# Decoder layer on one core: expert rows gathered five tiles ahead, and the long convolution's products formed from cyclic copies

## What is computed

```python
x = x + attn(layernorm(x))
# convolution: 32 heads of 8 channels, 256 taps, k = v = ctx, q = layernorm(x)
kv  = einsum('bhil,bhjl->bijhl', k_, v_)           # 8 x 8 products a head, symmetric in i, j
y   = causal_conv(kv, ssm_kernel) + kv * D         # each product along the sequence
out = einsum('bijhl,bhil->bjhl', y, q_)            # sum over i against q
x = x + out
# experts: top 2 of 8 by a softmax router
for e in range(8): inter += where(sorted_ids == e, rows, 0) @ expert_gate_up[e]
h = up * silu(gate);  out_rows = h @ expert_down[e];  out.at[token].add(out_rows * score)
x = x + out
```

## Time and profile before

| | us |
|---|---|
| median of 3 runs | 1803.71 (1803.37 to 1810.03) |
| the profiled execution, its own time | 1810.99 |
| its span, first to last instruction | 1809.1 |
| convolution: first matmul of the heads to the last, both groups | 743.1 to about 1134.9 |
| experts: first row transposes to the last down product | 1304.3 to 1797.6 |
| busy: PE, DVE, POOL, ACT | 1513.5, 1141.0, 712.3, 678.5 |

### The profile page before, as it was taken

The page is one execution under the profiler, slowest core; times in us unless marked ns, Lnnn a source line. Parts: engine busy times, 40 slices in busy tenths (PEclk is TensorE's granted clock), DMA queues, the critical chain, the costliest instruction groups (busy, mean ns, idle before and its releaser), DMA issues. The chain is left out here.

```text
span 1809.1 us, 34128 instructions
## 1 busy us (share of the span) xinstructions
PE 1513.5 (84%) x8665; PEld 1192.7 (66%) x8666; DVE 1141.0 (63%) x3591; ACT 678.5 (38%) x1818; POOL 712.3 (39%) x1160
## 2 busy tenths in 40 slices
PE   4999999999999997799968888667187888878886
PEld 4888888888888885666656666567155555555554
DVE  5788777777777776699989999866422222222221
ACT  3777677767676776100001000023122222222222
POOL 2111111111111101688846888266633343344343
PEclk9999999999999999999989999655599999899999
DMA  5543333433343445411131111369534444344441
GB/s 168 122 106 95 94 93 93 110 94 93 95 109 92 109 97 216 151 46 47 46 116 36 47 45 34 128 162 259 128 66 74 76 72 73 66 78 79 72 79 35
DMA packets 89767, 172.13 MB, mean 95 GB/s; under 512 B 26384, under 2 KB 26384, under 8 KB 88656
## 3 DMA queue, kind: packets, MB, share of 16 engines
q1 hardware_dynamic: 63584, 122.46, 25.3%
q0 software_dynamic: 18176, 35.80, 11.0%
q10 hardware_dynamic: 7920, 12.93, 2.8%
HBM read 78.10 MB, written 44.79 MB: 68 GB/s over the span
## 5 line engine op out<-in xcount | busy, mean ns | idle before, releaser
L1097 PE MATMUL ps_y<-pairs,taps 128*128 128x288 f32 x1280 | 324.5, 410 | 35.4 <-DVE prods L1170 32.1
L1097 PEld LDWEIGHTS ps_y<-pairs,taps 128*128 128x128 f32 x1280 | 238.3, 190 | 121.1 <-POOL pairs L1041 41.6
L853 ACT ACTIVATE probs<-neg_scores,neg_max 128x256 f32<-128x256 f32 x512 | 255.2, 505 | 26.1 <-DVE neg_max L654 25.9
L1170 DVE TENSOR_TENSOR prods<-ps_y,q_g 128x224 f32<-128x224 f32 (+7 forms) x960 | 251.3, 402 | 17.7 <-issue 8.0
L654 DVE CUSTOM_DVE_ANT_0 neg_scores<-ps_scores,alibi 128x256 f32<-128x256 f32 x512 | 194.8, 418 | 91.0 <-PE ps_scores L519 60.4
L1041 POOL TENSOR_TENSOR pairs<-ctx_g 128x32 f32 (+11 forms) x512 | 215.5, 460 | 43.0 <-PE ps_y L1097 31.8
L1513 POOL DMA_INDIRECT out<-y_row,back x72 | 113.2, 1573 | 293.1 <-ACT y_row L1705 158.3
L1894 DVE TENSOR_TENSOR st_lo<-ps_x,st_hi 128x512 fp32r<-128x512 f32 x72 | 49.8, 691 | 249.2 <-ACT st_hi L1690 249.2
L863 ACT ACTIVATE probs_t<-ps_probs_t 128x512 f32<-128x512 f32 x208 | 124.0, 596 | 130.5 <-PE ps_probs_t L530 130.4
L530 PE MATMUL ps_probs_t<-ident,probs 128*128 128x128 f32 x1024 | 159.2, 279 | 8.9 <-ACT probs L853 8.9
L1588 PE MATMUL ps_x<-ident,srow 128*128 128x128 f32 x288 | 49.1, 296 | 121.0 <-DMA srow<-xn_rows,take 120.8
(11 more groups left out here) (185 smaller groups left out, 3287.2 us busy)
## 6 DMA issues: line engine op xcount, KB each, us to landing
q_stack<-q_hi SPq DMA_DIRECT2D x128, 128.0 KB, 2.3
k_stack<-k_hi SPq DMA_DIRECT2D x128, 128.0 KB, 2.3
taps<-kernel_pad SPq DMA_DIRECT2D x64, 256.0 KB, 3.1
x_in<-in_x SPq DMA_DIRECT2D x16, 512.0 KB, 3.5
q_stack<-q_lo SPq DMA_DIRECT2D x64, 128.0 KB, 2.3
k_stack<-k_lo SPq DMA_DIRECT2D x64, 128.0 KB, 2.3
x_rows<-x_mid SPq DMA_DIRECT2D x16, 512.0 KB, 3.0
ctx_g<-in_ctx_t SPq DMA_DIRECT2D x2, 4096.0 KB, 12.4
```

Source lines behind the costliest of these rows:

```text
L853: last = act.activation(probs[h % 2][:, tt, :], neg_scores[h % 2][:, tt, :], ACT.Exp, bias=neg_max[par][:, h, tt:tt + 1], scale=-1.0, accu ...
L1097: last = pe.matmul(ps_y[par][:, lc, 0:GB * PAIRS], taps[r][:, block_cols:block_cols + P], pairs[par][:, mc, :, :], start=(mc == 0), stop=( ...
L1170: last = dve.tensor_tensor(prods[par][:, :, :, to:to + n, term], y[:, :, :, col:col + n], head_of(q_g, own, q_from, n), ALU.mult)
```

## The change

**Experts.** RING goes from 8 to 12, the rows have six buffers (`ROW_BUFS`) instead of four, and the gather runs five tiles ahead (AHEAD = 5) instead of three. The scatter of tile n now always waits for the landing of tile n-2, and for that of tile n-1 only where the two tiles have different experts: a table `tile_wait_i`, made by three more DVE instructions at the end of routing (and a constant made by POOL and DVE at its start), gives the value to wait for, which POOL loads into a register for each tile.

**Convolution.** The ring of eight is laid out twice in a row, so that a ring row that wraps is contiguous. Three tiles are new, each with two buffers: `ctx_ring` and `q_ring` (the head's eight values twice) and `y_rows` (each ring row of y continued by the values that a later row needs). ACT fills them: `turn_ctx` one copy, `keep_y` one copy for `q_ring` and three from `ps_y` for `y_rows`. POOL's `form_pairs` is two multiplications, of 1024 and 128 elements. DVE's `multiply` is four, of 1280 and three times 256 elements, from `y_rows` and `q_ring`; the result is term by term. DVE's `halve` adds terms 4 to 7 onto 0 to 3 (1024 elements), POOL's `fold` adds 2 onto 2 (512) and then 1 onto 1 (256), and signals `z_ready`. PE waits for ACT's copy (`y_kept`) where it waited for DVE.

```diff
                 def form_pairs(g, k, par):
                     pool.wait_ge(y_ready, k * 2 + (g * SH + par + 1 - 2 + Y_START))
-                    for col, i, j, n in pair_segments():
-                        last = pool.tensor_tensor(pairs[par][:, :, :, col:col + n],
-                                                  head_of(ctx_g, k * 2 + par, i, n),
-                                                  head_of(ctx_g, k * 2 + par, j, n), ALU.mult)
-                    last.then_inc(pairs_ready, 1)
+                    wait_apart(pool, ctx_ring_ready, k * 2 + (g * SH + par + 1), passed)
+                    own = by_lane(ctx_g, k * 2 + par)
+                    to = pairs[par][:, :, :, :].rearrange("p m b q -> p (m b) q")
+                    pool.tensor_tensor(to[:, :, 0:HALF * SD].rearrange("p n (d i) -> p n d i", i=SD),
+                                       own.unsqueeze(2).to_broadcast([P, EC * GB, HALF, SD]),
+                                       turned(ctx_ring[par], HALF), ALU.mult)
+                    pool.tensor_tensor(to[:, :, HALF * SD:PAIRS], own[:, :, 0:HALF], own[:, :, HALF:SD], ALU.mult)\
+                        .then_inc(pairs_ready, 1)
...
-                    wait_apart(pool, prods_ready, k * 2 + (g * SH + par + 1 + PRODS_START), passed)
-                    first = prods[par][:, :, :, :, 0:FOLD]
-                    pool.tensor_tensor(first, first, prods[par][:, :, :, :, SD - FOLD:SD], ALU.add).then_inc(folded, 1)
+                    h = k * 2 + (g * SH + par)
+                    wait_apart(pool, halved, h + 1, passed)
+                    pool.tensor_tensor(prods[par][:, :, 0:2, :], prods[par][:, :, 0:2, :], prods[par][:, :, 2:4, :], ALU.add)\
+                        .then_inc(folded, 1)
+                    wait_apart(pool, folded, h + 1, passed)
+                    pool.tensor_tensor(by_lane(q_g, k * 2 + par), prods[par][:, :, 0, :], prods[par][:, :, 1, :], ALU.add)\
+                        .then_inc(z_ready, 1)
...
-                    pe.wait_ge(prods_ready, h + (1 - 2 + PRODS_START))
+                    pe.wait_ge(y_kept, h + (1 - 2 + KEPT_START))
...
+                def keep_y(g, k, par):
+                    h = k * 2 + (par + g * SH)
+                    act.wait_ge(prods_ready, h + (1 - 2 + PRODS_START))
+                    ring_of(q_ring[par], q_g, k * 2 + par)
+                    act.wait_ge(y_ready, h + (1 + Y_START))
+                    y = ps_y[par][:].rearrange("p c (b q) -> p (c b) q", b=GB)
+                    near = y[:, :, 0:HALF * SD].rearrange("p n (d i) -> p n d i", i=SD)
+                    rows = y_rows[par]
+                    whole_rows = rows[:, :, 0:HALF * ROW].rearrange("p n (d r) -> p n d r", r=ROW)
+                    act.activation(whole_rows[:, :, :, 0:SD], near, ACT.Copy)
+                    act.activation(whole_rows[:, :, 0:HALF - 1, SD:ROW], near[:, :, 1:HALF, SD - HALF + 1:SD], ACT.Copy)
+                    act.activation(rows[:, :, HALF * ROW:ROWS].rearrange("p n (u i) -> p n u i", u=2),
+                                   y[:, :, HALF * SD:PAIRS].unsqueeze(2).to_broadcast([P, EC * GB, 2, HALF]),
+                                   ACT.Copy).then_inc(y_kept, 1)
...
+                    with act.Fori(0, SH // 2 - 1) as k:
+                        for par in range(2):
+                            keep_y(g, k, par)
+                            turn_ctx(g, k + 1, par)
...
                 def multiply(g, k, par):
-                    dve.wait_ge(y_ready, h + (1 + Y_START))
+                    dve.wait_ge(y_kept, h + (1 + KEPT_START))
                     dve.wait_ge(z_ready, h + (1 - 2 + Z_START))
...
+                    dve.tensor_tensor(prods[par][:, :, 0:HALF + 1, :], main_rows(y_rows[par], HALF + 1),
+                                      turned(q_ring[par], HALF + 1), ALU.mult)
+                    for e in range(HALF + 1, SD):
+                        d = SD - e
+                        last = dve.tensor_tensor(prods[par][:, :, e, :], y_rows[par][:, :, d * ROW - d:d * ROW - d + SD],
+                                                 q_ring[par][:, :, e:e + SD], ALU.mult)
                     last.then_inc(prods_ready, 1)
 
-                def add_up(g, k, par):
-                    wait_apart(dve, folded, k * 2 + (par + g * SH + 1), passed)
-                    dve.tensor_reduce(head_of(q_g, k * 2 + par, 0, SD), prods[par][:, :, :, :, 0:SD - FOLD], AX_X,
-                                      ALU.add).then_inc(z_ready, 1)
+                def halve(g, k, par):
+
+                    h = k * 2 + (par + g * SH)
+                    wait_apart(dve, prods_ready, h + (1 + PRODS_START), passed)
+                    dve.tensor_tensor(prods[par][:, :, 0:HALF, :], prods[par][:, :, 0:HALF, :], prods[par][:, :, HALF:SD, :],
+                                      ALU.add).then_inc(halved, 1)
...
-        RING = 8
+        RING = 12
         BUFS = 4
-        AHEAD = 3
+        ROW_BUFS = 6
+        AHEAD = 5
...
-                    if not (first_round(kk) and r == 0):
-
-                        wait_apart(pool, y_scattered[(r - 1) % BUFS], turn(kk, r - 1) * 16 + 16, passed)
+                    if not (first_round(kk) and r < 2):
+
+                        wait_apart(pool, y_scattered[(r - 2) % BUFS], turn(kk, r - 2) * 16 + 16, passed)
+                    if one_back:
+
+                        wait_apart(pool, y_scattered[(r - 1) % BUFS], landed, passed)
```

More of the change, by code:

```diff
@@ L1284, in build_decoder @@
                 back = [sb_in(tiling, f"back{i}", [P, 1], U32) for i in range(RING)]
[L1285 removed]
+                srow = [sb_in(tiling, f"srow{i}", [P, E]) for i in range(ROW_BUFS)]
                 st = [[sb_in(tiling, f"st_{part}{i}", [P, EC, P], F32R) for part in ("hi", "lo")] for i in range(2)]
@@ L1330, in build_decoder @@
             take_ready = sem("take_ready")
-            row_load = [sem(f"row_load{i}") for i in range(BUFS)]
+            row_load = [sem(f"row_load{i}") for i in range(ROW_BUFS)]
             st_done = sem("st_done")
```

116 lines of the change are left out of this document (75 added, 41 removed).

## The result

The kernel after takes 1946.22 us (median of 4 runs, 1944.21 to 1951.73), the kernel before on the same chip 1805.16 (1803.37 to 1810.03): a ratio of 1.078, interval 1.075 to 1.081. The prediction was 1932. The profiled execution of the kernel after took 1945.0, its span is 1943.3.

What follows compares the result with a forecast made beforehand. DVE was taken to bound the convolution at 5.65 us a head, and PE with late gathers the experts. Convolution +225 and experts -97 give +128, 1939 on the profiled basis, 1932 us as a median; range 1850 to 1990.

Steps and rivals of the forecast that it cites:

- Part 1: Experts: gathers five tiles ahead are hidden, PE sets 5.4 us a tile instead of 6.75, 97 us less.
- Part 2, engine costs: Convolution, work a head: DVE 3.8 us, POOL 4.7, ACT 1.8, PE 5.1.
- The chain of two heads: Convolution: loop through fold, pairs, PE, ACT, multiply, halve and fold takes 16.3 us over two heads, 8.1 a head.
- The exclusion: Convolution: DVE and POOL instructions on SBUF tiles run in turns, 8.8 us a head with two handoffs.
- PE's clock: Convolution: PE's clock falls in idle time, so slower bursts add 0.4 us a head, bounds 0 to 1.4.
- The sum of a head: Convolution: 9.2 us a head against 5.65, 220 us more over 62 steps.
- (a): Convolution: no exclusion and the clock stays up, 8.0 us a head, 1857 us; chance 0.10.
- (b): Convolution: every PE burst starts at lower clock, or POOL's strided operands cost more; 9.9 a head, 1975 us; chance 0.22.
- (c): Experts: transfers in flight slow each other, step 6.4 us, gain only 25, 2004 us in all; chance 0.07.
- (d): Convolution: no exclusion, POOL folds while DVE halves, PE sets 5.2 us a head, 1684 us; chance 0.04.
- (e): Whole kernel: both parts cancel, near 7.1 us a head, within 0.5% of before; chance 0.02.
- the signs the prediction named: Profile after: PE bursts 8.7 to 9.5 us apart, DVE idle about 2 before each first multiplication, expert steps 5.4.

Runs made afterwards that it cites:

- e8: Kernel before with only the experts' change, but each scatter waits for the landing of the scatter before it in every tile: 1725.14 us.
- e9: Kernel before with only the experts' change, but the gather three tiles ahead instead of five: 1810.39 us, ratio 1.003.
- e10: Experts of after; convolution keeps ring copies and two-instruction pairs, DVE multiplies from PSUM in eight stride-writing instructions and reduces six terms: 1697.31 us, ratio 0.937 to before.
- e3: Kernel after with DVE's halve of a head put right behind that head's multiply: 1830.43 us.
- e11_fill_16: Kernel after with 16 needless identity matmuls on PE ahead of every odd head's burst: 1893.01 us.
- e4: Kernel after with DVE's multiplications reading PSUM instead of SBUF (output wrong, only time read): 1893.16 us.
- e5: Kernel after with halve right behind its multiply and multiplications reading PSUM (output wrong, only time read): 1711.75 us.
- e6: Kernel after with 32 needless identity matmuls on PE ahead of every odd head's burst: 1938.95 us.

## Why the prediction was right, and where it wasn't

**Part 1, -97; measured -118.0, and 109 alone.** Right in mechanism: no wait for `srow`, POOL's added register load and wait hidden. (109 is a difference of medians; the profiled execution of before was 7 above its median.) The step was mis-sized, 5.18 for 5.40. Its base of 5.34 was the time from the row transposes to the modelled end of the down product; here the same stretch is 1749.39 + 1.88 - 1745.92 = 5.35, but the next tile starts 0.17 before that end. Matmul ends overlap what follows, and a step is start to start. 72 x 0.22 is 16 of the 21 us. Another 3 come from the step of before: 6.75 was read up to 1797.56, the end of the last down product but one, and from the row transposes of the third tile; from down product to down product it is 6.80.

**Which half gains** was not in the prediction. It put the gain down to the distance, and e8 and e9 agree (80 us, and nothing without it); the 30 us of the relaxed wait on top were not foreseen. POOL's 3.2 us a tile hold no wait for a landing; with the wait of every tile, as in e8, they are 5.5.

**Part 2, engine costs.** DVE 1.49 + 1.09 + 1.22 = 3.8 a head (3.8 predicted), POOL 2.28 + 0.46 + 1.27 + 0.72 = 4.7 (4.7), ACT 1.7 (1.8), PE 5.1 at full clock. All held. The reason given for DVE's 2.6 did not: it priced an instruction by elements and a start, as if the fifteen had been many starts. e10 has the same time with eight, so what the change saves on DVE is the stride, not the count. The sum came out because the rows of 1226 and 424 ns were contiguous ones; with the stride 1024 elements take 2.04 and not 1.23.

**The chain of two heads** held link by link. Predicted: pairs 2.7, PE 5.1, ACT 1.8, multiply 2.6 and halve 1.2, folds 2.0, handoffs 0.9, in all 16.3. In the two heads shown: pairs 3.93 (842.83 to 846.76), PE and its handoff 7.60 (827.38 to 834.98), ACT 1.69, multiply and halve 3.63 (836.79 to 840.42), folds 2.26 with 0.27 between, the other handoffs 0.33: 19.4. Beyond the 16.3 stand 1.2 for the pairs that met DVE and 2.5 for the slow burst, less 0.6 by which the copies, DVE and the handoffs were priced too high. Without both the chain is 17.05 - 1.25 = 15.8, or 7.9 a head. e3 proves the chain by taking it away.

**The exclusion** holds, but it was put into the sum in the wrong way. The prediction had two bounds, chain 8.1 and turns 8.8, and took the larger. In e3 the turns alone are 7.25, under the chain: 8.5 and two handoffs added lone durations, and the hidden starts are not in them. But turns and chain are no alternatives: where pairs and multiply meet, the wait lies on the chain and is added to it. e11_fill_16 has 8.5 a head where no burst is slow, so 8.8 was near by two errors that cancel, a bound that is too high and an addition left out. That is luck. The Trainium skill, page "SBUF — State Buffer", section "Who interferes with whom", was cited for a lock that lasts a whole instruction. The runs agree that the waiting one gets nothing until the other ends, and show besides that it then ends a little sooner than its lone time would have it.

**PE's clock** was under-priced: 0.4 a head taken, within bounds of 0 to 1.4; it is 1.2, of which e11_fill_16 gives back 53 / 62 = 0.86. The reason given for 0.4 was that most idle times of the experts cost nothing; but those are at most 3.1 us, and here every second burst began after 5.4 to 7 and took 6.5 to 8.2 instead of 5.1.

**The sum of a head.** Once a group is under way it is 9.68 against 9.2: 0.8 more for the clock, 0.3 less for the rest. With the quicker first heads the growth is 9.44 - 5.59 = 3.85 a head against 3.55, which over 62 heads is 19 of the 21 us by which +245.7 exceeds +225; the others lie at the groups' ends. Part 1 gained 21 more than forecast, so the two cancel, and that is luck too. With the 6.5 outside of both the spans differ by 134 instead of 128. The other 8 of the 14 us between 1932 and 1946 come from the profiled execution of before, which was 7.3 above its first median, while that of after is 1.2 under its own.

**Not in the prediction:** before the first head DVE normalizes rows for `xn_g` while POOL forms pairs, now in long instructions. DVE first, then POOL, from the timeline of after:

```profile
731.30 7.02 DVE L1216 TENSOR_SCALAR xn_g<-x_res,all_moments,all_rstd 128x512 f32 x6 [2.70 <-PEq L1097]
```

```profile
731.57 2.40 POOL L1059 TENSOR_TENSOR pairs<-ctx_g,ctx_ring 128x1024 f32<-128x1024 f32 x1 [12.43 <-ACT ctx_ring L1152]
```

Six of DVE's take 7.02 us, where two take 1.00 once POOL has ended its pairs, and where the same six took 5.06 from first start to last end in the kernel before. From the first of them to the first matmul of the heads it is 17.2 us instead of 14.3. So 2.9 of the 5.4 us by which the heads start later lie here, and 2.0 of these are the six. The other 2.5 stand already ahead of them, in the attention, which was not changed: the first of the six starts between 726 and 733 us in the profiled executions of these kernels.

**Rivals.** (a) had no exclusion: refused by the rows at 842.9. (b), 9.9 a head from a slow burst at every head or dear strides on POOL, was half true: only every second head has the slow burst, and POOL's operands cost no more than its rows had shown. (c) needed steps of 6.4. (d) and (e) needed 7.1 a head, which of e3, e4, e5, e6 and e11 only e5 passes. Of the signs the prediction named, one was half right: DVE waits for POOL's second fold only at every second multiplication, at the others for ACT.

## What to carry to other kernels

When work that one engine did with a single signal is spread over four, write down the loop that returns to the same buffer and sum its links; it was 15.8 us over two heads here, 19.4 with what disturbed it, with every engine under 5.2 a head, and no list of busy times shows it. Price two engines that exclude each other in turns only where they really meet, and add that wait to the loop, and price an idle PE on a chain by what its next burst costs. Take the halves of a change apart: here 109 us of gain from the experts' part stood under 250 of loss, and the kernel with that half alone (1695, ratio 0.938) beats both.

## What the runs showed of the hardware

- DVE operations on float32 with a stride of 32 bytes in SBUF, read or written, cost 1.9 to 2.0 ns an element instead of 1.1 to 1.2: a reduction of 1536 took 2.95 us against 1.75, a multiplication of 1024 written so 2.04 against 1.23. The Trainium skill, page "SBUF — State Buffer", section "Door 1: The DMA port swizzle", states lines of 16 bytes and a penalty for each access that crosses to a new one; at 32 bytes each does, and the rows agree.
- A DVE tensor_scalar on float32 that reads one SBUF tensor (and a scale and an offset for each partition) is held up by POOL's multiplications too: 7.02 us for six, against 0.50 each. The Trainium skill, page "SBUF — State Buffer", section "Who interferes with whom", counts tensor_scalar among the operations that can take the shared pair of ports; the rows agree.
- Instructions of DVE and POOL that exclude each other change over at the ends of instructions, and the later one ends 0.11 to 0.13 us sooner after the earlier than it would alone (fold 1.14 for 1.25, halving 1.09 for 1.22 in e3).
- A PE burst of twenty passes that begins after 5.4 to 7 us of idle time took 6.5 to 8.2 us instead of 5.1, and 3.7 us of needless matmuls in that gap gave back 53 us of 1946; 7.3 us of them gave back 7. After 2.2 to 2.5 us of idle time (e11_fill_16) a burst took 5.1 us at one time and 6.7 to 6.8 at another; the granted clock of 755 to 1000 was 0.81 in the kernel after and 0.95 there.
